# Diagonal blocks by transfer, small vector work on GpSimd and ScalarE, paired products: one change to a two-layer kernel on one core

## What is computed

```python
x = x + attn(_layernorm(x), ...)      # gated delta rule, 16 heads of 64
x = x + ffn(_layernorm(x), ...)       # softmax attention, 16 heads of 8, then experts

# attn, per head, token by token (q, k, v after a causal 4-tap convolution and silu; q, k rotated and normalised)
ot = qt @ S + D * sum(qt * kt) * vt
S  = at * (S - bt * kt (kt @ S)) + bt * kt vt
beta = sigmoid(x @ bw + bb); alpha = exp(-exp(A_log) * softplus(x @ gkw + gkb + dt_bias))
out = ((x @ Wg) * silu(rmsnorm(o) * onorm_w)) @ Wo

# ffn: attention over all 256 tokens, then 8 experts of 512 units, all computed, weights of the best 2 kept
probs = softmax(xt @ Wg); wts, idx = top_k(probs, 2); h1 = gelu(xt @ W1[e] + b1[e]); ye = h1 @ W2[e] + b2[e]
```

## Time and profile before

| | |
|---|---|
| median of 3 runs | 5545.79 us (5541.89 to 5554.14) |
| the profiled execution | 5533.59 us, span 5531.7 us |
| PE busy | 4792.2 us (87%) |
| PEld (weight loads) busy | 3609.5 us (65%) |
| DVE busy | 4623.1 us (84%) |
| ACT busy | 3445.0 us (62%) |
| POOL busy | 2085.5 us (38%) |
| mean granted TensorE clock | 0.843 of 2.4 GHz |
| DMA | 197.13 MB, 36 GB/s |

### The profile page before, as it was taken

One profiled execution on the slowest core, in us unless ns is written; L12 is line 12 of the kernel. 1 busy time (PEld: TensorE's weight loads), 2 busy tenths in 40 slices (PEclk: granted clock), 3 DMA queues, 4 the chain that ended last, 5 costly groups with the idle time before them and its releaser, 6 DMA issues.

```text
span 5531.7 us, 111231 instructions
## 1 busy us (share of the span) xinstructions
PE 4792.2 (87%) x40448; PEld 3609.5 (65%) x40448; DVE 4623.1 (84%) x11457; ACT 3445.0 (62%) x6166; POOL 2085.5 (38%) x1485
## 2 busy tenths in 40 slices
PE   4688889988889898889898899888899888899986
PEld 2466667666667666667666677666677666677665
DVE  6888898888888888988888988888988888988852
ACT  3456666656666656766666666566666666666653
POOL 3443333443343442343443344433434433334420
PEclk7778898888888888988888888878988888888878
DMA  1001111011111011111111111111111011111011
GB/s 59 10 11 34 43 43 34 28 32 37 43 43 34 24 32 41 43 33 32 33 33 42 43 33 32 32 34 43 43 34 32 32 34 43 43 34 32 31 34 56
DMA packets 214453, 197.13 MB, mean 36 GB/s; under 512 B 13848, under 2 KB 176416, under 8 KB 209696
## 3 DMA queue, kind: packets, MB, share of 16 engines
q1 hardware_dynamic: 213920, 190.01, 11.1%
HBM read 148.02 MB, written 4.19 MB: 28 GB/s over the span
## 4 chain that ended last, share of the span: by engine, by line
DVE 52%; PE 38%; issue 8%; ACT 1%; SPq 0%; DMA 0%; POOL 0%; DVEq 0%; POOLq 0%; ACTq 0%
PE bank L984 36%; DVE acc L1390 10%; DVE tmpb L1556 6%; DVE NP L1526 6%; DVE Gam L1559 5%; DVE mx L1653 3%; DVE Gam L1512 3%; DVE moe L1738 2%; PE bank L988 2%; DVE QK L1671 1%; DVE QK L1479 1%; DVE Gam L1563 1%; DVE rot L1475 1%; DVE ms L1603 1%; DVE Kt L1543 1%
## 5 line engine op out<-in xcount | busy, mean ns | idle before, releaser
L1390 DVE SCALAR_TENSOR_TENSOR acc<-bank,conv_w,acc 128x255 f32<-128x255 f32 (+2 forms) x2304 | 925.1, 470 | 27.3 <-ACT acc L791 26.4
L717 POOL TENSOR_TENSOR sq<-acc 128x256 f32<-128x256 f32 x256 | 191.2, 747 | 1734.5 <-ACT acc L797 1722.3
L984 PE MATMUL bank<-QK 64*128 64x256 f32 (+1 forms) x4096 | 603.3, 352 | 211.8 <-DVE mx L1653 97.7
L984 PE MATMUL bank<-W,h 128*128 128x128 f32 x4096 | 579.7, 302 | 190.1 <-issue 103.3
L984 PEld LDWEIGHTS bank<-W,h 128*128 128x128 f32 x4096 | 551.7, 215 | 237.1 <-issue 129.6
L984 PE MATMUL bank<-mT,W 128*128 128x256 f32 x2048 | 626.4, 447 | 60.3 <-issue 39.7
L984 PEld LDWEIGHTS bank<-QK 64*128 64x128 f32 (+1 forms) x4096 | 288.6, 142 | 523.7 <-issue 346.0
L966 ACT ACTIVATE h<-bank,b 128x256 f32<-128x256 f32 x1024 | 416.7, 479 | 288.6 <-PE bank L984 286.7
L984 PEld LDWEIGHTS bank<-mT,W 128*128 128x128 f32 x2048 | 420.9, 220 | 219.2 <-issue 155.3
L729 POOL TENSOR_TENSOR rot<-rot,sin 128x512 f32<-128x512 f32 x256 | 337.3, 1317 | 450.8 <-DVE rot L1475 450.8
L1559 DVE TENSOR_TENSOR Gam<-Gam,tmpb 128x31 f32<-128x31 f32 (+15 forms) x992 | 448.1, 452 | 34.1
(11 more groups left out here) (226 smaller groups left out, 10275.4 us busy)
## 6 DMA issues: line engine op xcount, KB each, us to landing
W<-in_W SPq DMA_DIRECT2D x512, 256.0 KB, 3.2
QK<-QK SPq DMA_DIRECT2D x32, 1024.0 KB, 5.1
xin<-in_x SPq DMA_DIRECT2D x32, 128.0 KB, 4.7
x<-in_x SPq DMA_DIRECT2D x32, 128.0 KB, 2.1
...
```

The lines of the kernel that those rows point to most:

```text
L984: return mm(out_, lhsT, rhs, start=first, stop=last)
L1390: v.scalar_tensor_tensor(acc[:, n % 2, m, j:T], ps[:, m, 0:T - j], conv_w[:, kind, c, PAD - j:KT - j], acc[:, n % 2, m, j:T], ALU.mult, AL ...
```

## The change

- **Diagonal blocks.** `diag` leaves ScalarE. After each `fac` SP issues eight transfers from `NP` to `Dg`, one for each of four row groups and two chunks: 32 partitions, 4 units, 32 numbers (128 bytes) a piece. That is 32 transfers for a sequence. `Dg` is laid out unit by unit now, and `blocks` reads it with a stride.
- **To GpSimd:** the rotation's eight additions; the gate's polynomial, now 18 instructions; the third part of the q and k split; the split of the maxima, now six instructions.
- **To ScalarE:** four of the copies that split alpha, and two of the q and k split. VectorE keeps the subtractions.
- **Fewer:** a factor moves into the square's scale, which drops one small VectorE instruction per chunk (L1609).
- **Paired products.** `rep`, `max` and `st` are one step for two heads, whose products are issued alternately. The two heads lie in different rows of TensorE's array (0 to 63 and 64 to 127; for `rep` groups of 32). A step opens two banks at once.
- **Order.** All five lists and the banks are new. The greatest lag is 4 where it was 3.

```diff
     "sp": """
-        xnG:0@1 x1:0@3 expert:1@3 expert:0@3 expert:2@3 expert:3@3 expert:4@3 expert:5@3 QK1:0@1 store:0@3 expert:7@3
-        expert:6@3 xin:0@0""",
+        expert:7@4 store:0@4 expert:0@3 xnG:0@1 expert:1@3 x1:0@3 diag:0@1 QK1:0@1 diag:1@1 xin:0@0 expert:2@3 diag:2@1
+        diag:3@1 expert:3@3 expert:4@3 expert:5@3 expert:6@3""",
...
+REP_PAIRS = ((0, 2), (1, 3), (4, 6), (5, 7))
...
-        Dg = over(Gam, 0, [SB, NU])
+        Dg = over(Gam, 0, [NU, SB])
...
+            def diagonal(i, n):
+                sp.wait_ge(v_Kt.sem, v_Kt.at(i, n + 1))
+                for q in range(P // SB):
+                    for t in range(NT):
+                        units = slice(t * H + 4 * n, t * H + 4 * n + 4)
+                        sp.dma_start(Dg[ROWS[q], units, :], NP[ROWS[q], units, 1, ROWS[q]]).then_inc(diag_in.sem, 16)
...
+            def turned(k, c):
+                pool.wait_ge(p_rope.sem, p_rope.at(k, 2 * c + 2))
+                g.tensor_tensor(chunk(c), chunk(c), by_token(rot[:, c % 2]), ALU.add).then_inc(p_QK.sem, 1)
...
+                for m, d in enumerate((11, 9, 7, 5, 3, 1)):
+                    pool.wait_ge(p_gate.sem, p_gate.at(i, 2 + 2 * m))
+                    g.tensor_tensor(lpp[:], lpp[:], lp2[:], ALU.mult).then_inc(p_gate.sem, 1)
+                    pool.wait_ge(p_gate.sem, p_gate.at(i, 3 + 2 * m))
+                    g.tensor_scalar(lpp[:], lpp[:], 1.0 / d, None, ALU.add).then_inc(p_gate.sem, 1)
...
+                pool.wait_ge(a_part.sem, a_part.at(j, 2))
+                g.tensor_tensor(part[:, 2], prest[:], part[:, 1], ALU.subtract).then_inc(p_part.sem, 1)
...
-                for q in range(P // SB):
-                    units = NP[ROWS[q], :, 1, ROWS[q]].rearrange("p (t h) k -> p k t h", t=NT)
-                    ins = s.copy(Dg[ROWS[q]].rearrange("p k (t h) -> p k t h", t=NT)[:, :, :, heads - 4:heads],
-                                 units[:, :, :, heads - 4:heads])
...
+                    s.copy(al1[:], a_t).then_inc(a_al.sem, 1)
+                    s.copy(alpha3[0:H, :, 2:GW], a_t[:, :, 1:P]).then_inc(a_al.sem, 1)
+                else:
+                    act.wait_ge(v_alpha.sem, v_alpha.at(i, 1))
+                    s.copy(al2[:], alr[:]).then_inc(a_al.sem, 1)
+                    s.copy(alpha3[32:32 + H, :, 2:GW], alr[:, :, 1:P]).then_inc(a_al.sem, 1)
...
-                for t in range(NT):
-                    ins = product(pair(ps)[:, t, :], QK6[rows, c, 0, TOK[t]], QK6[rows, c, 1, :])
-                ins.then_inc(full("max", n), 1)
+                for t in range(NT):
+                    for n in both:
+                        rows = rows_of(n)
+                        ins = product(pair(bank("max", n))[:, t, :], QK6[rows, c, 0, TOK[t]], QK6[rows, c, 1, :])
+                        if t == NT - 1:
+                            ins.then_inc(full("max", n), 1)
...
-                dve.wait_ge(a_diag.sem, a_diag.at(i, 4))
-                v.transpose(Eb[:], Dg[:]).then_inc(v_blk.sem, 1)
+                dve.wait_ge(diag_in.sem, diag_in.at(i, 16 * 32))
+                v.transpose(Eb[:], Dg[:].rearrange("p u k -> p k u")).then_inc(v_blk.sem, 1)
```

More of the change, by code:

```diff
@@ L971, in _ @@
                 "square": squares_of, "sums": sums_copy, "vtap": first_tap_v, "vsilu": silu_v, "vcopy": values,
-                "diag": diagonal, "upper": upper, "join1": first_join, "join2": second_join, "top": solved_top,
+                "upper": upper, "join1": first_join, "join2": second_join, "top": solved_top,
                 "low": solved_low, "S": state, "osq": square, "g": gates, "osilu": silu_o, "yT": turned_y,
@@ L975, in _ @@
                 "att": probabilities, "context": context, "ctxT": turned_ctx, "mT": turned_m, "ex": router,
-                "gelu": gelu})
+                "gelu": gelu, "al": alpha_parts, "part": parts})
         @block.tensor
```

338 lines of the change are left out of this document (174 added, 164 removed).

## The result

The changed kernel takes **4960.48 us** (median of 4 runs, 4945.52 to 4975.57) against 5543.84 for the kernel before, measured with it (5531.1 to 5554.14): ratio 0.8949, 95% interval 0.8914 to 0.8983.

The account below looks back on a forecast made before the run. PE and DVE were taken to bound the turn alternately: PE in the chain, DVE outside. 60 + 99 = 159 us a turn for 165.95, scaled to 5302 and then 5315 us; range 5080 to 5540.

Parts of the forecast that it names:

- chain, `close` to `o:3`: Stretch of each turn where PE holds the end: 50.4 us, forecast to grow to 60 by added PE work.
- outside it: Rest of the turn, `alpha:0` to `close`, held by DVE: 115.6 us, forecast to fall to 99.
- I let half of the early rise pay: In the chain, half the gain from 2.4 GHz returning earlier offsets added products at 1.2 GHz and a little more: 60 us.
- The fillers: PE steps newly placed in the chain, `down:7` and `pv:3` among them: about 11 us, or 22 at 1.2 GHz.
- rival 1: The clock comes back early and the chain hardly grows: chain 53, rest 97, 150 us a turn, 5013 us; chance 0.20.
- up to 8 us: In the chain, the most that an earlier return to 2.4 GHz was said to be worth per turn.
- I cut one turn: Stretch lengths and busy times came from one profiled turn: 50.4 us from `close` to `o:3`, 115.6 for the rest.
- 13 us lost: In the profiled turn's chain, PE ran about 26 us at half clock, said to lose some 13 us.
- I take 2 us off: Outside the chain, 101 us became 99 for fewer GpSimd waits and fewer GpSimd instructions beside the elimination.
- a meeting with GpSimd: An elimination instruction on DVE slowed beside GpSimd work: 0.4 us or more each; by the skill's rule up to 1.3.
- Wait about nothing: `blocks` waits about nothing for the diagonal's transfers: 8.2 us for eight, against 8.1 us of DVE work in the gap.
- at nothing: `diag:2` queued on SP behind `expert:2`'s wait was costed at nothing, that product coming some 8 us before `fac:3`.

Follow-up runs that it names:

- down_late: Changed kernel with `down:7` moved from right behind the joins to some 12 us later in the chain, before `qk:4`: 5091.71 us.
- down_early: Changed kernel with `down:7` moved one place up, ahead of the joins, where TensorE stood idle waiting for `close`: 5025.43 us.
- The fills: Changed kernel plus useless GpSimd work beside the elimination: memsets 4958.43 us, short multiplications 5032.94 us, longer multiplications 5082.06 us.
- diag3_split: Changed kernel with four of the last diagonal quarter's eight transfers issued from ScalarE's queue, four still from SP's: 4921.95 us.
- unpaired: Changed kernel with `rep`, `max` and `st` issuing one head's products together, then the other's, instead of alternating: 4956.0 us.
- rope_dve: Changed kernel with the rotation's eight additions put back on VectorE: 5105.03 us.
- old_diag_act: The change's instructions in the previous kernel's order and banks, without alternation, ScalarE again copying the diagonal blocks: 5743.52 us, 1.0376 of the kernel before.

## Why the prediction was wrong

| term, us a turn | forecast | measured |
|---|---|---|
| chain, `close` to `o:3` | 60, from 50.4 | 54.2, from 53.5 (means of 23) |
| outside it | 99, from 115.6 | 94.1, from 113.4 |
| DVE in all | 133.1 | 4123.1 / 32 = 128.8 |
| elimination's relief | under 2 | 6.0 |
| wait for the diagonal | 0, at most 3 to 5 | 1.6 |
| strided read of `blocks` | +0.7 | 1.91 for 1.24 |
| ACT, POOL in all | 3000, 2650 | 3032, 2636 |

**Chain.** The step that failed is "I let half of the early rise pay". The fillers came in as counted, 11 us. But 2.4 GHz returned after 14 us instead of about 29, as in rival 1, and paid almost in full. Two lines of before at half clock, not shown so far, then the same work in the changed kernel, show how much:

```profile
2683.29 1.97 PE L984 MATMUL bank<-V,Z 64*64 64x64 f32 x16
...
2698.33 1.98 PE L984 MATMUL bank<-Gam,Kt 128*64 128x64 f32 x32
```

```profile
2532.32 3.78 PE L1060 MATMUL bank<-W,h 128*128 128x128 f32 x16
...
2538.79 1.14 PE L1060 MATMUL bank<-V,Z 64*64 64x64 f32 x16
...
2549.53 1.15 PE L1060 MATMUL bank<-Gam,Kt 128*64 128x64 f32 x32
```

In the turn of the earlier trace rows, some 22 us of such work ran at 1.2 GHz, at 1.97 for 1.14 us: as an estimate, 9 to 10 lost. Now `down:7` (3.78 for 2.02), a `kT` and half of a `pv` do: about 2.7 lost. With 10: 50.4 + 11 - 7.3 = 54.1. For that turn "up to 8 us" was right and halving it was not. `down_late` and `down_early` show that the place of `down:7` brings the early return.

There is a second fault beneath it, "I cut one turn". Its chain of 50.4 us was one of the shortest of the 23; in the median one 2.4 GHz returned after 38 us, not 29. In the mean the early rise gave back 53.5 + 11 - 54.2 = 10.3 us, nearly all that the fillers cost. The forecast let the chain grow by 9.6 us, and it grew by 0.7: of the 11 us a turn that the forecast missed by, about 9 lie here. The "13 us lost" of the prediction was too high for its own turn, since the 32 x 32 joins cost the same at either clock (below), and about right for the mean one (10.3 + 2.7).

**Outside.** The step that failed is "I take 2 us off". I priced a meeting with GpSimd by a mean, 0.43 us, and then counted the instructions that enter, not those that leave. Before, 15.1 us of GpSimd work stood there, two `vscale:0/1` of 1.96 us among it, and 6.7 stand there now. The fills price it: one moved `vscale` costs 1.5 us, 8.1 us in pieces of 1.3 cost 4.3. With two `vscale` at 1.5 and some 4 us of long pieces at 0.5 a microsecond, that makes about 5 of the 6.0, as an estimate; the rest isn't isolated. Another 1.7 us is again the turn that was cut: DVE was busy 109.3 us outside its chain, and 107.6 in the mean of 23. The rule of the Trainium skill (SBUF — State Buffer, section "SBUF: two separate sides") that I weighed against the row has the mechanism right. It spoke for this change, since more reading leaves the elimination than enters.

**Diagonal.** "Wait about nothing" was 1.6 us, because `diag:2` was held by `diag:1`, `xin` and `expert:2`, and 16 transfers stood in a row. I costed that queue "at nothing". What I didn't see at all is the other side of it, PE's wait for weights, 87.3 us for 19.3 before. It cost little here, since without it and without the wait of `blocks` `diag3_split` gained 0.8 us a turn.

**What held.** The alternation is worth nothing on the path (`unpaired`). The GpSimd polynomial is hidden in most turns, and costs 1.1 us in 8 of 32. VectorE's moved work counts outside the chain alone (`rope_dve`), and outside it the time fell by 19.3 us a turn with 18.4 us less of DVE's work: that picture of the prediction stands, with a larger number. Rival 1, 53 + 97, came nearest, and it too had the second part too high. What the prediction didn't say is that the gain hangs on the order: the same moved work in the old order (`old_diag_act`) relieves DVE by 3.6 us outside the chain and is slower than before.
